# Batch 0's keys of a gated WKV and FFN layer: formed from raw x by a diagonal matrix and a product of two rows on TensorE

## The reference, cut to what matters

```python
# WKV over the tokens of a batch, per channel, with k = ln(x), v = ctx and a decay w < 0 or > 0
y_t = (sum_{s<t} exp(w*(t-1-s) + k_s) * v_s + exp(u + k_t) * v_t) / (the same without v)   # written there as a scan
x = x + tanh(g_xattn) * y
D = gelu(float16(ln(x)) @ W0.T + bias0) -> float16      # 1024 -> 4096
E = D @ W1.T + bias1 -> float16                         # 4096 -> 1024
out = x + tanh(g_ffn) * E
```

## Time and profile before

| | us |
|---|---|
| median of three runs | 1927.05 (1925.21 to 1929.18) |
| the profiled execution's own time | 1929.11 |
| its span in the profile | 1927.3 |
| TensorE busy with matmuls | 1824.5 (95%) |
| VectorE busy | 882.2 (46%) |
| ScalarE busy | 574.9 (30%) |
| GpSimd busy | 335.0 (17%) |
| mean granted TensorE clock | 0.988 |

### The profile page before, as it was taken

The page is one execution under the profiler, slowest core; times in us unless marked ns, Lnnn a source line. Parts: engine busy times, 40 slices in busy tenths (PEclk is TensorE's granted clock), DMA queues, the critical chain, the costliest instruction groups (busy, mean ns, idle before and its releaser), DMA issues.

```text
span 1927.3 us, 21556 instructions
## 1 busy us (share of the span) xinstructions
PE 1824.5 (95%) x8920; PEld 881.4 (46%) x8920; DVE 882.2 (46%) x1053; ACT 574.9 (30%) x721; POOL 335.0 (17%) x349
## 2 busy tenths in 40 slices
PE   1688699999999999999999999999999999999999
PEld 0467544444444444444444444444444444444444
DVE  8788729899347858733214776741300000000000
ACT  6748324643333434311002434420101111200000
POOL 6543202555321212100000221110000000000000
PEclk9989799999999999999999999999999999999999
DMA  7595566866664353324343452333233212223330
GB/s 272 183 317 195 202 216 239 291 229 227 223 185 169 106 178 145 131 89 137 126 154 136 144 173 104 120 131 120 89 131 125 88 50 88 88 74 101 131 120 33
DMA packets 91149, 291.97 MB, mean 151 GB/s; under 512 B 13862, under 2 KB 26150, under 8 KB 83884
## 3 DMA queue, kind: packets, MB, share of 16 engines
q1 hardware_dynamic: 83132, 177.30, 27.8%
q10 hardware_dynamic: 7920, 113.30, 16.6%
HBM read 223.41 MB, written 67.16 MB: 151 GB/s over the span
## 4 chain that ended last, share of the span: by engine, by line
PE 77%; DVE 11%; ACT 4%; issue 4%; POOL 3%; DMA 1%; SPq 0%; DVEq 0%; POOLq 0%; ACTq 0%
PE accs L1124 38%; PE accs L1102 36%; DVE S L884 3%; PE accs L1083 1%; POOL W L568 1%; DVE S L872 1%; DVE S L875 1%; DVE stats L784 1%; POOL X L544 1%; DVE front L870 1%; ACT L653 1%; DVE front L853 1%; DVE front L881 1%; DVE front L878 1%; ACT L704 1%
## 5 line engine op out<-in xcount | busy, mean ns | idle before, releaser
L1124 PE MATMUL accs<-DT,W 128*128 128x512 f16 x4096 | 888.4, 380 | 0.0
L1102 PE MATMUL accs<-XT,W 128*128 128x512 f16 x3584 | 776.0, 380 | 1.1 <-ACT XT L662 1.1
L1124 PEld LDWEIGHTS accs<-DT,W 128*128 128x128 f16 x4096 | 401.4, 98 | 489.5 <-issue 10.1
L1102 PEld LDWEIGHTS accs<-XT,W 128*128 128x128 f16 x3584 | 351.1, 98 | 425.4 <-issue 2.4
L929 DVE SCALAR_TENSOR_TENSOR xo<-e,tg,xo 128x512 f32<-128x512 f16 x64 | 50.2, 785 | 635.8 <-ACT e L720 635.8
L712 ACT ACTIVATE DT<-accs,small 128x512 f16<-128x512 f32 x224 | 154.0, 688 | 490.9 <-PE accs L1102 490.4
L720 ACT ACTIVATE e<-accs,small 128x512 f16<-128x512 f32 x64 | 43.9, 685 | 654.8 <-PE accs L1124 653.1
L884 DVE RECIPROCAL S<-front 128x512 f32<-128x512 f32 (+1 forms) x72 | 215.6, 2994 | 0.0
L544 POOL TENSOR_TENSOR X<-X,S 128x512 f32<-128x512 f32 (+1 forms) x72 | 94.0, 1305 | 492.6 <-DVE S L887 492.6
L870 DVE TENSOR_TENSOR front<-front,V 128x512 f32<-128x512 f32 (+1 forms) x72 | 45.8, 636 | 135.1 <-ACT front L653 135.1
L568 POOL TENSOR_TENSOR W<-stage,W 128x1024 f16<-128x1024 f32 x41 | 86.7, 2128 | 60.3 <-ACT stage L696 60.3
(11 more groups left out here) (92 smaller groups left out, 873.3 us busy)
## 6 DMA issues: line engine op xcount, KB each, us to landing
W<-parts_dram ACTq DMA_DIRECT2D x54, 2048.0 KB, 9.2
stage<-w_in SPq DMA_DIRECT2D x52, 512.0 KB, 5.2
parts_dram<-W SPq DMA_DIRECT2D x94, 256.0 KB, 5.2
xin<-x_in SPq DMA_DIRECT2D x32, 512.0 KB, 6.9
x_dram<-X SPq DMA_DIRECT2D x32, 512.0 KB, 3.8
xo<-x_dram SPq DMA_DIRECT2D x32, 512.0 KB, 4.2
out<-xo SPq DMA_DIRECT2D x32, 512.0 KB, 9.1
V<-vT_in SPq DMA_DIRECT2D x56, 256.0 KB, 5.2
```

Of the source, the lines that this page charges most:

```text
L1102: mm = nc.tensor.matmul(acc[m % BANKS], W[:, (nb // Q) % 2, part, nb % Q, P * c:P * (c + 1)], XT[:, c, HALF * half:HALF * (half + 1)], sta ...
L1124: mm = nc.tensor.matmul(acc[m % BANKS], W[:, s % 2, part, q, P * c:P * (c + 1)], DT[:, nb, HALF * half:HALF * (half + 1)], start=(nb == 0 ...
```

## The change

- Keys of batch 0: ScalarE makes a diagonal matrix of rstd for each tile (`diag_x`, 128x128), and TensorE multiplies the raw tile by it in float32 (`key_pieces`). Ahead of it in the same bank stands a product of two rows (`key_row`): [1; max(w, 0)] by [-mean x rstd; -token]. The first row of the right-hand factor comes from the column `offset` by a product with the identity (`row_x`) and a copy by ScalarE (`lift_row`). `norm_x`, `lessen_x` and the broadcast load of w are gone; one row of w is loaded on ScalarE's queue.
- Units: tanh(g) moves from the last product (L887) to the product with v (L870) and to the seeds. GpSimd waits for tanh(g) and multiplies the seeds by it ahead of its first `seed`.
- The seam ahead of slot 0: ScalarE does the second `norm_x2`, into a bank of its own for the transposes.
- Pieces: nine with the units (12 before), three `BEHIND`, 13 in slots 0 to 24, seven from slot 33 on. Of pieces 14, 17, 20, 23 and 25 to 31 GpSimd does the scaled float32.
- Units and residuals of batch 0 stand in earlier slots.

```diff
-    for i, (k, a) in enumerate(((1, 5), (1, 8), (3, 10), (3, 13), (8, 16), (8, 19), (13, 21), (13, 24))):
+    for i, (k, a) in enumerate(((0, 4), (0, 7), (1, 9), (1, 12), (7, 14), (7, 17), (12, 19), (12, 22))):
-    for i, (k, a) in enumerate(((31, 36), (32, 41), (37, 46), (42, 50), (47, 55), (51, 60), (56, 63), (61, 63))):
+    for i, (k, a) in enumerate(((28, 33), (29, 37), (34, 42), (38, 46), (43, 51), (47, 55), (52, 60), (56, 63))):
-WITH_UNIT = ((0, 1), (2,), (3, 4), (5,), (6, 7), (8,), (9, 10), (11,))
-BEHIND = (12, 13, 14)
-PREP_SLOT = {15 + j: 1 + 2 * j for j in range(LAG - 15)}
-PREP_SLOT.update({LAG + j: 34 + 3 * j for j in range(NB - LAG)})
+WITH_UNIT = ((0,), (1,), (2,), (3, 4), (5,), (6,), (7,), (8,))
+BEHIND = (9, 10, 11)
+PREP_SLOT = {12 + j: 2 * j - j // 6 for j in range(LAG - 12)}
+PREP_SLOT.update({g: s for g, s in zip(range(LAG, NB), (33, 35, 37, 40, 43, 46, 49))})
+BY_POOL = (14, 17, 20, 23) + tuple(range(LAG, NB))
...
+            pool.wait_ge(s_pool0, 10)
+            pool.wait_ge(s_act0, 1)
+            nc.gpsimd.tensor_tensor(seeds[:, :, :, 0], seeds[:, :, :, 0],
+                                    tg[:, 0:1].to_broadcast([P, B * CB]).rearrange("p (b c) -> p b c", b=B),
+                                    ALU.mult).then_inc(s_pool0, 1)
...
+                if g in BY_POOL:
+                    pool.wait_ge(hi_done, g + 1)
+                    nc.gpsimd.tensor_scalar(staged, staged, W_SCALE, None, ALU.mult).then_inc(ws_done, 1)
...
+            def diag_x(T):
+                act.wait_ge(rstd_done[0], T + 1)
...
+                nc.scalar.activation(diag[:, T % HT, :], ident[:, :], ACT.Copy, scale=rstd[:, 0, T % 2, 1:2])\
+                    .then_inc(diag_done, 1)
+            def lift_row(ch):
+                act.wait_ge(row_done, (2, 4, TILES)[ch])
...
             for T in range(2):
-                norm_x(T)
+                diag_x(T)
+            lift_row(0)
             for n in range(CB):
                 exps(n)
                 for g in WITH_UNIT[n]:
                     hi_piece(g)
-            hi_piece(BEHIND[0])
-            norm_x(2)
+            diag_x(2)
+            norm_x2(1)
+            diag_x(3)
             copy_xt(0)
             copy_xt(1)
-            norm_x(3)
-            for g in BEHIND[1:]:
+            lift_row(1)
+            for g in BEHIND:
                 hi_piece(g)
...
-                nc.vector.tensor_tensor(EV, E, values, ALU.mult).then_inc(ev_done, 1)
+                nc.vector.scalar_tensor_tensor(EV, E, tg[:, 0:1], values, ALU.mult, ALU.mult).then_inc(ev_done, 1)
...
             stats_x(2)
             stats_x2(0)
-            offset_x(2)
             stats_x2(1)
             norm_x2(0)
+            offset_x2(1)
+            offset_x(2)
             stats_x(3)
-            norm_x2(1)
-            lessen_x(2)
             offset_x(3)
-            lessen_x(3)
...
                         stats_x2(3)
                         norm_x2(2)
-                        norm_x(4)
+                        offset_x(4)
                         stats_x(5)
                         norm_x2(3)
-                        lessen_x(4)
                         for T in range(5, 8):
-                            norm_x(T)
+                            offset_x(T)
                             if T < 7:
                                 stats_x(T + 1)
-                            lessen_x(T)
...
+            def key_row(n):
+                ch, c = divmod(n, CB)
+                nc.tensor.matmul(unit_banks(n)[0], ones_w[:, P * c:P * (c + 1)], lift_of(ch), start=True, stop=False)
+            def key_pieces(n):
...
+                for j, T in enumerate(tiles):
+                    mm = nc.tensor.matmul(bank[:, P * j:P * (j + 1)], xin[:, T % HT, P * c:P * (c + 1)],
+                                          diag[:, T % HT, :], start=False, stop=(T == tiles[-1]))
+            def row_x(T):
+                pe.wait_ge(offset_done, T + 1)
...
+                nc.tensor.matmul(row_bank(ch)[:, P * j:P * (j + 1)], offset[:, T:T + 1], ident[:, :],
+                                 start=True, stop=True).then_inc(row_done, 1)
...
+            for T in range(2):
+                row_x(2 + T)
             for T in range(2):
                 channels_x2(T)
...
                         channels_x2(2)
                         channels_x2(3)
+                        for T in range(HT, TILES):
+                            row_x(T)
```

More of the change, by code:

```diff
@@ L582, in _ @@
             for n in range(CB):
-                lo_piece(WITH_UNIT[n][0])
+                if n < CB - 1:
+                    for g in WITH_UNIT[n]:
+                        lo_piece(g)
                 residual(n)
-                for g in WITH_UNIT[n][1:]:
-                    lo_piece(g)
+            for g in WITH_UNIT[CB - 1]:
+                lo_piece(g)
             rstd_of(0, 2)
@@ L649, in exps @@
                     act.wait_ge(s_dve0, 6)
-                lack = 1 if b and h else 0
+                lack = h
                 bank = unit_banks(n)[0]
@@ L656, in copy_xt @@
                 act.wait_ge(xt_done, T + 1)
-                tile = T
                 if T == HT:
@@ L694, in hi_piece @@
                 nc.scalar.activation(hi, staged, ACT.Copy, scale=W_SCALE).then_inc(hi_done, 1)
-                act.wait_ge(hi_done, g + 1)
-                nc.scalar.activation(ring[slot], ring[slot], ACT.Copy, scale=W_SCALE).then_inc(ws_done, 1)
+                if g not in BY_POOL:
+                    act.wait_ge(hi_done, g + 1)
+                    act.wait_ge(ws_done, g)
+                    nc.scalar.activation(ring[slot], ring[slot], ACT.Copy, scale=W_SCALE).then_inc(ws_done, 1)
             def gelu_early(m):
@@ L750, in _ @@
                     if K == SECOND:
+                        diag_x(4)
                         copy_xt(2)
                         copy_xt(3)
+                        for T in range(5, 8):
+                            diag_x(T)
+                        lift_row(2)
                     if K == THIRD:
@@ L774, in _, with stats_of @@
         def _(dve):
-            def stats_of(i, T, halves, free):
+            def stats_of(i, T, halves):
                 if i == 0 and T >= TILES + 2:
                     dve.wait_ge(norms_stored[T % 2], 16 * ((T - TILES) // 2))
+                elif i == 0 and T >= 2:
+                    dve.wait_ge(offset_done, T - 1)
+                    dve.wait_ge(diag_done, T - 1)
                 elif T >= 2:
-                    dve.wait_ge(free, T - 1)
+                    dve.wait_ge(xh_ready, T - 2)
+                    dve.wait_ge(xh1_ready, 1)
                 if T >= 1:
@@ L823, in stats_x2 @@
                 rows = token_banks(T)
[L824 removed]
+                stats_of(1, T, [rows[:, 0, :], rows[:, 1, :]])
             def norm_x2(T):
@@ L1031, in unit @@
                 elif ch == 2 and c < 2:
-                    pe.wait_ge(xh_ready, 3 + c)
+                    pe.wait_ge(xh_ready, 2 + c)
                 else:
                     pe.wait_ge(y_done, n - 1)
-                for T in tiles:
-                    mm = transpose_piece(n, T)
-                mm.then_inc(kt_done, 1)
+                key_row(n)
+                key_pieces(n)
             def token_piece(T, c):
@@ L1128, in quarter2 @@
                     mm.then_inc(mm_done, 1)
-            pe.wait_ge(s_pool0, 7)
+            pe.wait_ge(s_pool0, 9)
             for T in range(2):
-                pe.wait_ge(xn_ready, T + 1)
-                for n in range(2):
-                    mm = transpose_piece(n, T)
-                    if T == 1:
-                        mm.then_inc(kt_done, 1)
+                row_x(T)
+            pe.wait_ge(lifted, 1)
+            for n in range(2):
+                key_row(n)
+            pe.wait_ge(diag_done, 2)
+            for n in range(2):
+                key_pieces(n)
             for n in range(2, CB + 2):
```

134 lines of the change are left out of this document (76 added, 58 removed).

## The result

The kernel after the change takes 1941.7 us (median, 1937.07 to 1944.4), the one before 1927.05: a ratio of 1.0072 [1.0055, 1.0088]. It is slower by 14.65 us. The forecast was 1928.0, the range 1922.5 to 1934.0, so the result lies outside it and above it. The profiled execution after is the median itself: 1941.7 us, 1.8 above its span of 1939.9. The spans differ by 12.6 us; the other 2 us are the distance that the profiled execution of before had from its median.

What follows compares the result with a forecast made beforehand. TensorE, at 77% of the span, was taken to bound the kernel, only the 244.5 us ahead of slot 64 counting. +5.3 + 1.84 + 1.45 - 6.78 - 0.9 = +0.9 us gave 1928.0 us, range 1922.5 to 1934.0.

Steps and rivals of the forecast that it cites:

- the scaling's price in slots 0 to 24: Slots 0 to 24: GpSimd's scaling taken at 1.1 us; group 24 ends 5.3 us later, start and seam included.
- Rival D: Slots 0 to 24: scaling at 2.13 us, group 24 ends at 126.7, time 1929.8; counted with the forecast, together 0.48.
- my walk: Slots 0 to 24: engine queues reckoned in order, piece 24 done at 123.1 us, group 24 ending at 124.85 instead of 119.55.
- worth nothing: Units 0 to 7: nine pieces beside them instead of twelve free ScalarE and GpSimd, not the bound there; no gain.
- The start and the seam: Ahead of group 0: start gains 1.6 us, seam takes 13.05 against 11.63, group 0 starts at 65.75 instead of 64.14.
- Unit products in slots 25 to 63: Slots 25 to 63: eight units' row and four pieces at 1.7 us each add 10.1 us; stage +1.45 in all.
- rival B: Slots 25 to 63: float32 passes cost more than 0.11 us; 1932 at 0.17, 1943 at 0.35; chance 0.18.
- the stage ahead of slot 25: Four row products, the last needing tile 7's offset, delay group 25: 14.6 us against 12.76, +1.84.
- no wait for low parts in slots 25 to 63: Slots 25 to 63: four to six slots of lead instead of three remove 8.0 us in seven waits.
- unit 23 in time: Ahead of slot 64: unit 23 moves to slot 56, so TensorE's wait for its residual goes, -6.78 us; 1.4 to spare.
- rival A: Slots 0 to 24: the pieces keep up, group 24 ends at 119.55 as before; faster, 1922.7 us; chance 0.22.
- rival C: Ahead of slot 64: unit 23 is late again, 3 to 5 us of the wait stay, 1931 to 1933; chance 0.12.

Runs made afterwards that it cites:

- the lead alone: The kernel before with pieces 25 to 31 split from slot 33 on, four to six slots ahead, and loads two slots later: 1921.08 us, 0.9966.
- the kernel that beats both: The kernel before with pieces 25 to 31 split sooner, units 16 to 23 earlier and float16 filler products ahead of slots 25 and 64: 1912.69 us, 0.9931.

## Why the prediction was wrong

**The step that failed first is the scaling's price in slots 0 to 24**: "I take 1.1: one input lies nearer to the first". It is 2.77, outside the bounds of 1.1 and 2.13, and the run with two inputs gives 1.89. With the scalings back on ScalarE the kernel is 9.4 us faster. Both bounds came from rows of another kind: a write-only pass and a subtraction of two inputs. One was no floor for a scaling and the other, in the end, no ceiling. The sentence on the Trainium skill (GPSIMD Engine Reference, Engine selection: one input roughly at line rate) pointed the same wrong way, and this trace speaks against it: VectorE's clip of 128x1024 float32 took 0.69 us before the change, GpSimd's of 2x1024 takes 2.77; the same section's advice against elementwise work on GpSimd is what held. Rival D, the dearer end, gave only +1.9, since in my walk ScalarE didn't wait for GpSimd.

**A wait that I did not list**: the change adds `act.wait_ge(ws_done, g)`, so ScalarE waits for GpSimd's scaling. Without that wait slots 0 to 24 are 2.6 us shorter (4.2 by the medians, which alone don't tell it). My walk through the slots had no such wait. Behind TensorE's last wait came the half clock of groups 23 and 24, about 3 us, which I had not counted either: a wait on TensorE costs more than its own length.

The rest of that step comes out near: with the scaling on ScalarE the run shows three last waits, 4.2 us, and the stage took 57.8 us against my 59.1. My "Even with a free GpSimd the last two pieces cost about 2.9" wasn't tried as such, since in that run ScalarE had the work. That the nine pieces with the units were "worth nothing" is wrong as well: they cost 2.9 us.

**The start and the seam**: 4.6 us short. I took float32 prices from rows at full clock and believed the clock column, 1.00 from 15 to 52 us. The durations say otherwise: two transposes took 0.69 us there, sixteen 1.97 elsewhere. I had rows 12 in hand and used it as the far end of a rival instead of as the local price. At twice my prices the start gains nothing (13.75 + 1.7 = 15.45, against 15.35 before) and the two units in slot 0 cost 3.4; 4.43 was measured. The other part of the start is the clip on GpSimd, for which the prediction had no term: tanh(g) comes 0.73 us later. My sentence that the trace speaks against the Trainium skill's rule on transposes (TensorE: Matmul & The Clock Gate, Part 4) rested on the same column and falls with it. What that rule says isn't decided by this case, for the float32 products that took the transposes' place ran at half speed at the start as well.

**Unit products in slots 25 to 63**: 2.14 us instead of 1.7, eight times, 3.5 us. That is what was missed there (3.35): 1.1 us more of half clock and 1.0 us more of old waits gone nearly cancel. A row of 1.05 instead of 0.85, pieces at 0.125 a pass instead of 0.105, and 0.09 in the group behind. That is rival B in its mildest form: the sign didn't hang on it.

**Right, by the profile**: the stage ahead of slot 25 (14.66, forecast 14.6, with the row product waiting for VectorE's last offset at 149.76); no wait for low parts in slots 25 to 63, which by itself is worth 5.8 us on the old kernel; unit 23 in time, the wait of 6.78 gone, the transposes at 1.91; rival A was refuted by 16 us at slot 24's end, and rival C by the missing wait. Without the front's new division and the scalings on GpSimd 1929.4 was measured, near my 1928.0, but that is luck: group 0 is 4.3 us later than I had it and slots 25 to 63 take 2.8 more, while slots 0 to 24 take 6.1 less, because TensorE's late start finds its pieces ready, and the end 2.0 less.

## What to carry to other kernels

Price an operation on an engine by a row of the same kind on that engine; if there is none, the bounds from other kinds are not bounds, and the range has to say so. When work moves to another engine, list each wait that the counting of semaphores adds on the engine it leaves. And split a change whose parts sit in different stages: the lead alone is worth 5.8 us here, the new keys cost 10.8, the scalings on GpSimd 9.4 and the nine pieces instead of twelve 2.9, and together they read as one small loss. When stages have moved, look for a wait at its place in the program and not at its time in the other trace.

## What the runs showed of the hardware that I had not expected

- On GpSimd an in-place scaling of 128x1024 float32 by an immediate takes 2.77 us, the product with a broadcast column 1.89, the subtraction with a float16 result 2.13. An operation with an immediate (the clip) takes 2.77 also for two partitions by 1024.
- The clock column reads 1.00 where TensorE's durations are those of half speed: up to group 0, in the profile of before and of after. The same product (row of 256 columns) took 1.22 at 68.23 and 0.69 at 73.87, and the run with fillers at the start reads 0.50 from 20 to 50 us over the same lengths. Durations of like operations are the better witness.
- Fillers of float16 products bring the products behind them to full speed at the start (key pieces 1.16 instead of 2.08 for eight passes), and, in the kernel that beats both, hold the clock at 1.00 through stages that had 0.73 and 0.60. Group 0 stayed at 3.48 us behind them all the same; why isn't shown.
